# A vision block on one core: the second layer norm's first two groups ahead of the last third of the attention, the queries and keys of the second attention in 222 and 370 columns, unrotated scores first for four images

## The reference, cut to what matters

```python
h = tok(x)                                    # ternary weights, 8-bit activations
y = layernorm(h); q, k, v = split(y @ Wqkv)   # 16 heads of 16
num = exp(rotate(q) @ rotate(k).T / 4)        # rotated queries and keys
den = sum(exp(q @ k.T / 4))                   # unrotated ones, over all keys
h = h + where(causal, num / den, 0) @ v @ Wout + bout
x2 = layernorm(h)
q, k, g = x2 @ w_q, x2 @ w_k, sigmoid(x2 @ w_gate)   # 8 heads of 64, 8 experts
gm = one_hot(argmax(g)) * g
values = sum over e of gm[e] * (x2 @ value_experts[e])
o = softmax(causal(q @ k.T / 8)) @ values
h = h + sum over e, heads of (gm[e] * o) @ output_experts[e]
```

## Time and profile before

| | |
|---|---|
| runs | 240.1, 241.33, 242.55 us |
| profiled execution | 240.91 us, its span 238.4 us |
| PE busy | 207.9 us (87%) |
| DVE busy | 178.7 us (75%) |
| ACT, POOL busy | 93.7 and 79.5 us |
| mean granted clock of TensorE | 0.979 of full speed |

### The profile page before, as it was taken

The page is one execution under the profiler, slowest core; times in us unless marked ns, Lnnn a source line. Parts: engine busy times, 40 slices in busy tenths (PEclk is TensorE's granted clock), DMA queues, the critical chain, the costliest instruction groups (busy, mean ns, idle before and its releaser), DMA issues.

```text
span 238.4 us, 5151 instructions
## 1 busy us (share of the span) xinstructions
PE 207.9 (87%) x2079; PEld 179.6 (75%) x2079; DVE 178.7 (75%) x324; ACT 93.7 (39%) x184; POOL 79.5 (33%) x82
## 2 busy tenths in 40 slices
PE   0153969689979799999999999999999999999994
PEld 0033849688865689987677777778989999999993
DVE  1679895998977767933558666775799979979972
ACT  3578739958741335445332155156202022110000
POOL 8562677000443424002253564955661000000000
PEclk9999999979999679999999999999999999999999
DMA  6998000000000010001602006067005435532102
GB/s 177 265 302 322 2 0 4 0 3 3 3 3 3 18 71 3 0 0 29 252 3 88 3 12 254 0 181 201 3 7 185 120 123 172 165 95 61 44 0 103
DMA packets 7181, 19.56 MB, mean 82 GB/s; under 512 B 1043, under 2 KB 1878, under 8 KB 7030
## 3 DMA queue, kind: packets, MB, share of 16 engines
q1 hardware_dynamic: 7158, 19.24, 26.3%
HBM read 18.55 MB, written 0.68 MB: 81 GB/s over the span
## 4 chain that ended last, share of the span: by engine, by line
PE 49%; DVE 28%; issue 9%; ACT 4%; POOL 4%; DMA 4%; SPq 1%; DVEq 0%; ACTq 0%; POOLq 0%
PE ps L265 13%; PE ps L266 11%; PE ps L267 11%; DVE gx L1101 7%; DMA tw<-tok_weight 4%; PE ps L1233 3%; PE ps L1274 2%; PE ps L1434 2%; DVE oelo L1075 2%; DVE rden L930 2%; DVE amax L774 1%; PE ps L1404 1%; ACT ptb L720 1%; DVE stat L803 1%; POOL velo L485 1%
## 5 line engine op out<-in xcount | busy, mean ns | idle before, releaser
L1101 DVE TENSOR_TENSOR gx<-maskb,oT 128x1184 fp32r<-128x1184 bf16 x31 | 42.3, 1414 | 0.6 <-PE ps L267 0.6
L1038 DVE COPY_PREDICATED v<-onehot,ps 128x512 f32<-128x512 uint8 (+3 forms) x40 | 25.7, 661 | 17.6 <-PE ps L267 17.3
L265 PE MATMUL ps<-gx,oelo 128*128 128x296 f32 x124 | 37.8, 305 | 0.6 <-DVE gx L1101 0.6
L267 PE MATMUL ps<-gx,oehi 128*128 128x296 f32 x124 | 37.2, 300 | 0.0
L266 PE MATMUL ps<-gx,oehi 128*128 128x296 f32 x124 | 37.0, 298 | 0.0
L265 PE MATMUL ps<-vehi,x2lo 128*128 128x512 f32 (+3 forms) x90 | 35.2, 392 | 0.0
L266 PE MATMUL ps<-velo,x2hi 128*128 128x512 f32 (+3 forms) x90 | 33.3, 370 | 0.0
L267 PE MATMUL ps<-vehi,x2hi 128*128 128x512 f32 (+3 forms) x90 | 33.2, 369 | 0.0
L485 POOL TENSOR_TENSOR velo<-veraw,vehi 128x1024 fp32r<-128x1024 f32 x8 | 19.1, 2390 | 23.8 <-ACT vehi L657 17.3
L265 PEld LDWEIGHTS ps<-gx,oelo 128*128 128x128 f32 x124 | 23.3, 188 | 1.8 <-issue 1.3
L266 PEld LDWEIGHTS ps<-gx,oehi 128*128 128x128 f32 x124 | 23.4, 189 | 0.0
(11 more groups left out here) (165 smaller groups left out, 479.8 us busy)
## 6 DMA issues: line engine op xcount, KB each, us to landing
maskb<-mask_rows SPq DMA_DIRECT2D x32, 148.0 KB, 3.9
veraw<-value_w SPq DMA_DIRECT2D x8, 512.0 KB, 3.7
oeraw<-output_w SPq DMA_DIRECT2D x8, 512.0 KB, 4.0
xp<-x_rows SPq DMA_DIRECT2D x6, 336.0 KB, 9.9
w2raw<-w_qkgate SPq DMA_DIRECT2D x1, 1088.0 KB, 14.1
tw<-tok_weight SPq DMA_DIRECT2D x1, 768.0 KB, 8.4
wqraw<-w_qkv SPq DMA_DIRECT2D x1, 768.0 KB, 12.0
out<-yo SPq DMA_DIRECT2D x4, 148.0 KB, 1.9
```

Source lines behind the costliest of these rows:

```text
L265: pe.matmul(o, llo, rhi, start=start, stop=False)
L267: return pe.matmul(o, lhi, rhi, start=False, stop=stop)
L1038: dve.copy_predicated(v2[0:m, t, h0:h1], bcast(onehot[0:m, t, h0:h1, e], 2, DH2), ps[0:m, JBANK[n], 0:(h1 - h0) * DH2].rearrange("p (a b) ...
L1101: dve.tensor_tensor(gx[:, k % NGR].rearrange("p a b t -> p a (b t)"), bcast(maskb[:, w % NMR, k % MEU], 1, 2), oT[:, c % 2].bitcast(F32), ...
```

## The change

The diff, cut to its core; the line numbers in it are not those of the profile.

```diff
+        def unit(b, kind):
+            return 2 * b + (kind if b else 1 - kind)
...
-        NOP = (NB - 1) * BI * S // R
-        OPB = [(4 + g // 2, g % 2 * D) if g < NOP else (1, (g - NOP) * D) for g in range(G)]
-        D_ORDER = [("turn", 0), ("turn", 1), ("turn", 2), ("gate", 0), ("qk", 0), ("out", 4), ("out", 5),
-                   ("qk", 1), ("turn", 3), ("qk", 2), ("qk", 3), ("turn", 4), ("qk", 4), ("turn", 5),
-                   ("gate", 1), ("qk", 5), ("qk", 6), ("gate", 2), ("qk", 7), ("gate", 3), ("qk", 8),
-                   ("gate", 4)]
-        D_ORDER += [("qk", n) for n in range(9, 4 * C2)]
+        EARLY = 2
+        FRONT = EARLY * R
+        QKT = [slice(0, FRONT), slice(FRONT, T)]
+        NQ2 = 2 * C2
+        QKB = [(7, 0, 1)[n % 3] for n in range(NQ2)] + [4 + n % 4 for n in range(NQ2)]
+        OPB = [(7, 0), (7, D), (4, 0), (4, D), (6, 0), (6, D)]
+        OP_AFTER = [2, 2, 3, 3, NB, NB]
+        DENB = [5, 7, 5, 5]
+        D_ORDER = [("pv", NB - 1), ("turn", 0), ("turn", 1), ("qk", 0), ("qk", 1), ("den", NB - 1), ("out", 2), ("out", 3),
+                   ("qk", 2), ("qk", 3), ("out", 4), ("out", 5), ("qk", 4), ("turn", 2), ("qk", 5), ("qk", 6),
+                   ("turn", 3), ("qk", 7), ("gate", 0), ("gate", 1), ("turn", 4), ("gate", 2), ("turn", 5),
+                   ("qk", 8), ("gate", 3), ("qk", 9), ("gate", 4)]
+        D_ORDER += [("qk", n) for n in range(10, 2 * NQ2)]
...
+            for n in range(2):
+                pool.wait_ge(sm["rope_t"], RSTEPS * (n + 1))
+                w2_lo(n)
+            pool.wait_ge(sm["en_ready"], 2)
+            w2_lo(2)
             pool.wait_ge(sm["en_ready"], 2 * 2)
-            w2_lo(0)
-            pool.wait_ge(sm["en_ready"], 2 * 3)
-            w2_lo(1)
-            pool.wait_ge(sm["yT_ready"], 2)
-            w2_lo(2)
             w2_lo(3)
...
-            for n in range(NPJ - 2):
+            for n in range(NPJ - 3):
                 proj_read(n)
+            exps(0, 1)
+            proj_read(NPJ - 3)
+            exps(0, 0)
+            proj_read(NPJ - 2)
+            proj_read(NPJ - 1)
             def ve_hi(e):
                 act.wait_ge(ve_in[e % NVR], 16 * (e // NVR + 1))
@@ -657,13 +674,11 @@
                 act.activation(vehi[:, e % NVR], veraw[:, e % NVR], ACT.Copy).then_inc(sm["vehi_ready"], 1)
             for b in range(NB):
-                exps(b, 0)
-                if b == 0:
-                    proj_read(NPJ - 2)
-                    proj_read(NPJ - 1)
-                exps(b, 1)
-                if b < NVR:
-                    ve_hi(b)
...
+                if b:
+                    exps(b, 0)
+                    exps(b, 1)
+                if 1 <= b <= NVR:
+                    ve_hi(b - 1)
...
-            for b in range(1, NB - 1):
-                causal(b)
-                denominators(b - 1)
-                normalise(b - 1)
-            denominators(NB - 2)
-            normalise(NB - 2)
-            causal(NB - 1)
+            causal(1)
+            denominators(0)
+            normalise(0)
+            causal(2)
+            denominators(1)
+            normalise(1)
+            causal(3)
...
             ln_apply(1, 1)
             x2_lo(0)
+            x2_lo(1)
+            denominators(2)
+            normalise(2)
+            denominators(3)
+            normalise(3)
+            residual(2)
             ln_apply(1, 2)
-            x2_lo(1)
+            residual(3)
             x2_lo(2)
-            denominators(NB - 1)
-            normalise(NB - 1)
-            residual(3)
             ln_apply(1, 3)
             residual(4)
+            x2_lo(3)
             residual(5)
             ln_apply(1, 4)
-            x2_lo(3)
             ln_apply(1, 5)
             x2_lo(4)
             x2_lo(5)
...
+                u = unit(b, kind)
+                if kind:
+                    pe.wait_ge(sm["keys_zero"], 1)
+                    pe.wait_ge(sm["act_read"], act_reads(PJ.index(("qk", late - 1, KC - 1, 1))))
+                else:
+                    pe.wait_ge(sm["keys_zero"], 2)
+                    pe.wait_ge(sm["rope_t"], RSTEPS * KC * late)
+                if u == 0:
                     bank_free(NEARLY - 1)
                 for t in range(2):
-                    if b + kind:
-                        pe.wait_ge(sm["exp_ready"], 4 * b + 2 * kind + t - 1)
+                    if u:
+                        pe.wait_ge(sm["exp_ready"], 2 * u + t - 1)
...
+                if b == NB - 1:
+                    pe.wait_ge(sm["rden_ready"], NB - 1)
+                pe.wait_ge(sm["exp_ready"], 2 * unit(b, 1) + 2)
...
                 if b == 0:
+                    scores(0, 1)
+                    scores(0, 0)
                     proj_job(NPJ - 2)
                     proj_job(NPJ - 1)
+                    denominators(0)
+                    continue
+                scores(b, 0)
+                if b == 1:
+                    attend(0)
                 else:
                     denominators(b - 1)
+                if b == NB - 1:
+                    for g in range(EARLY):
+                        out_proj(g)
                 scores(b, 1)
-                if b == NB - 1:
-                    out_proj(0)
-                    out_proj(1)
-                    denominators(b)
-                    for g in range(2, NOP):
-                        out_proj(g)
-                attend(b)
+                if b < NB - 1:
+                    attend(b)
...
+                before = [m for m in range(n) if QKB[m] == QKB[n]]
+                if before:
+                    pe.wait_ge(sm["qk2_ready"], before[-1] + 1)
+                elif QKB[n] == 7:
+                    pe.wait_ge(sm["h1_ready"], EARLY)
+                elif QKB[n] < 2:
+                    pe.wait_ge(sm["exp_ready"], 4 * NB)
+                elif QKB[n] == 4:
+                    pe.wait_ge(sm["h1_ready"], 2 * EARLY)
+                elif QKB[n] == 5:
                     pe.wait_ge(sm["yT_ready"], NB)
                 else:
-                    pe.wait_ge(sm["qk2_ready"], n - 3)
+                    pe.wait_ge(sm["h1_ready"], G)
                 base = (NQ if kind == "k" else 0) + c * P
-                tc = slice(hf * HALF, (hf + 1) * HALF)
-                pe.wait_ge(sm["x2lo_ready"], 3 if hf == 0 else G)
+                tc = QKT[hf]
+                pe.wait_ge(sm["x2lo_ready"], G if hf else EARLY)
```

More of the change, by code:

```diff
@@ L183, in vit_block @@
         yT = sbuf(proj, "yT", [P, KC, TP], F32, "right")
+        ed = sbuf(proj, "ed", [QR, RT, KC, BI, JS, S], F32, "right")
         en = sbuf(proj, "en", [QR, 2, 2, RT, KC, 2, JS, S], F32, "right")
-        ed = sbuf(proj, "ed", [QR, RT, KC, BI, JS, S], F32, "right")
         proj.close()
@@ L212, in vit_block @@
         ptb = sbuf(last, "ptb", [P, NT, NH2, TI_MAX, S])
-        yo = sbuf(last, "yo", [P, KC, 2, HALF])
         qk = ExitStack()
@@ L217, in vit_block @@
         qk.close()
+        yo = sbuf(last, "yo", [P, KC, 2, HALF])
         NOR, NOE = 4, 2
@@ L486, in ve_lo @@
                                    ALU.subtract).then_inc(sm["velo_ready"], 1)
-            for g in range(GI):
+            for g in range(EARLY):
                 rstd_of(1, g)
-            pool.wait_ge(sm["x2lo_ready"], GI)
+            pool.wait_ge(sm["x2lo_ready"], EARLY)
             ve_lo(0)
-            for g in range(GI, G):
+            for g in range(EARLY, G):
                 rstd_of(1, g)
@@ L681, in qk2_evac @@
                 act.wait_ge(sm["qk2_ps"], n + 1)
-                src, col = ps[:, 4 + n % 4, 0:HALF], slice(hf * HALF, (hf + 1) * HALF)
+                col = QKT[hf]
+                src = ps[:, QKB[n], 0:col.stop - col.start]
                 if kind == "k":
@@ L929, in denominators @@
                 dve.wait_ge(sm["den_ps"], b + 1)
-                dve.reciprocal(rden[:], ps[:, 5 + 2 * (b % 2), 0:UN * S]).then_inc(sm["rden_ready"], 1)
+                dve.reciprocal(rden[:], ps[:, DENB[b], 0:UN * S]).then_inc(sm["rden_ready"], 1)
             def normalise(b):
@@ L1243, in attend @@
                         pe.wait_ge(sm["en_ready"], 2 * b + ii // 2 + 1)
-                    if b == NB - 1 and ii == 2:
-                        turn_x2(0)
                     for c in range(KC):
@@ L1260, in denominators @@
                 for j in range(JP):
-                    ins = pe.matmul(ps[32 * j:32 * j + 32, 5 + 2 * (b % 2), 0:UN * S], cols("blk2", QR),
+                    ins = pe.matmul(ps[32 * j:32 * j + 32, DENB[b], 0:UN * S], cols("blk2", QR),
                                     ed[:, j // JS, :, :, j % JS], start=True, stop=True)
@@ L1265, in out_proj @@
             def out_proj(g):
-                if g < NOP:
+                if g == 0:
                     pe.wait_ge(wout_in, 16)
-                    pe.wait_ge(sm["yT_ready"], NB - 1)
-                else:
+                elif g == G - 1:
                     pe.wait_ge(sm["yT_pad"], 1)
-                    pe.wait_ge(sm["yT_ready"], NB)
```

(41 more changed lines are left out.)

10 lines of the change are left out of this document (2 added, 8 removed).

## The result

The changed kernel takes 250.28 us (median of 4 runs, 249.92 to 252.57) against 240.72 us (median of 4, 238.61 to 242.55): **4.35% slower**, ratio 1.0435 with an interval of 1.0358 to 1.0511. The ratio leaves out executions more than 1.5% above the fastest of their kernel; by the medians it is 4.0%. The forecast was 241.4 us, no change.

A forecast was written before the change was run, and what follows sets the result against it. No engine was taken to bound the whole; DVE bounds the first attention, PE the stretch from 59.15 us. From 240.91, minus 1.2 for earlier value jobs, plus 0.6, 0.7 and 0.4 for clock falls: 241.4 us, no change; range 239.1 to 243.6.

The forecast's parts named there:

- two signs of being wrong: Forecast is wrong if DVE isn't full in the first attention, or if `x2_lo(5)` comes 2 us from 91.4.
- Front: Start of the attention: unrotated scores first let the fourth rotation start at 53.87 instead of 54.41, gaining 0.54 us on DVE.
- First residual at 69.15: Behind the two-group output projection: first residual starts at 69.15 instead of 72.43, 3.3 us earlier.
- clock term (a): PE lull from 56.5 to 59.1 us: a clock fall costs 0 to 1.7 us, taken as 0.6.
- clock term (b): PE lull from 71.6 to 76.6 us, short transposes and two jobs: costs 0 to 1.7 us, taken as 0.7.
- Four groups behind it: Groups 2 to 5 behind the last normalisation: `x2_lo(5)` ends at 91.4 instead of 91.83, 0.4 us of gain left.
- Tail: Behind `x2_lo(5)`, 8 jobs of 370 columns and 2 gate jobs: 9.5 us, value jobs at 100.9 instead of 102.14.
- clock term (c): PE lull from 86.6 to 91.5 us, gate jobs and transposes: costs 0 to 1.7 us, taken as 0.4.
- Rival 4: First attention: `w2_lo` steps collide with the rotations, 3 x 0.42 us on a full DVE; 242.7 us, chance 0.08.
- Rival 3: Every PE lull costs the clock in full, 1.1 to 1.7, 0.9 and 1.7 us; 244.0 us, chance 0.12.
- Rival 1: The clock holds in all three PE lulls; 239.7 us, chance 0.25.
- The sum of 1.2 us: Whole stretch ahead of the value jobs: they start at 100.9 instead of 102.14, 1.2 us earlier, before clock costs.

The follow-up runs named there:

- experiment 8: Kernel before with unused 512-column matmuls in its own lulls, ten ahead of the first scores, eight among transposes, gate and query jobs: 238.28 us, ratio 0.9925.
- experiment 9: Changed kernel with the old attention front and unused matmuls in all its lulls: 238.78 us, ratio 0.994.
- experiment 10: Changed kernel with all three PE lulls filled by unused matmuls, run once more: 238.81 us, ratio 0.9953.
- experiment 4: Kernel before with the new front of the attention alone: 246.95 us, ratio 1.0231.
- experiment 5: Changed kernel with fourteen unused 512-column matmuls right behind `attend(1)`, inside the low stretch: 248.24 us, ratio 1.0325.
- experiment 1: Changed kernel with ten unused 512-column matmuls in PE's wait ahead of `attend(1)`: 241.81 us, ratio 1.004.
- experiment 7: Changed kernel with 22 unused 64-column matmuls ahead of `attend(1)` instead of ten of 512: 246.54 us, ratio 1.0213.
- experiment 3: Changed kernel with the old front of the attention, rest of the change kept: 243.55 us, ratio 1.0123.
- experiment 6: Changed kernel with three unused 512-column matmuls ahead of `attend(1)` instead of ten: 239.69, 245.42 and 249.23 us.
- experiment 2: Changed kernel with all three PE lulls filled by unused matmuls: 239.07 us, ratio 0.9895.

## Why the prediction was wrong, point by point

- **What bounds the stretch**: right up to `causal(1)`, where DVE was full and PE waited. Behind it PE bounded, as forecast, but so much longer that DVE idled 3.66 and 2.46 us. The prediction's own two signs of being wrong both came: DVE wasn't full, and `x2_lo(5)` came 7 us from 91.4.
- **Front, 0.54 us on DVE**: right in the profile. The run is 0.63 us late from its start (the second rotation begins at 44.45 instead of 43.82), and `causal(1)` starts at 58.90, so 0.6 earlier against that. It was no gain of the order: the idle stretch that it removes was itself a loss to the low level, and a filled kernel before has none (experiments 8 to 10).
- **The wait moves to 56.5, 2.6 us**: right, 57.1 with that start, 2.67 us. (From 51.9 the terms given add up to 56.65; the 0.15 changes nothing.)
- **First residual at 69.15**: 75.72, and 68.70 with the wait filled. This is where it failed.
- **The step that failed: the clock term (a), "it costs between 0 and 1.7 us (3.4 at half speed)"**, taken as 0.6. It cost 5.9 us (75.72 less 0.63 less 69.15). I took the length of the low stretch from the row behind the old wait and didn't ask what ended that one: two dense projections. Behind the new wait stand 13 us of scores, products of the exponentials with the values or with the constants (`en`,`vblk` and `ed`,`cst`), and these did not raise the clock (experiments 4 and 5): it stayed low for 13.7 us, until 1.8 us into the output projection, instead of 3.4. So the upper bound of 1.7 us was no bound. That the wait moves and that the clock can fall behind it was right; the size of the term was wrong. The price of the level was off too: the 2.47 us of the earlier trace rows were partly at full clock; wholly at the low level the scores take 3.00.
- **Two groups' norm, 5.4 us from the first residual to `x2_lo(1)`**: right, 75.72 to 81.1.
- **Late batches, clock term (b)**: `x2_lo(1)` to the last normalisation was put at 5.25 us and took 6.6, so 1.3 instead of 0.7, inside its bounds.
- **Four groups behind it, 11.5 us**: 10.8 (87.70 to 98.46), where experiment 1 has 11.5. Why it is shorter here is not worked out.
- **Tail, 9.5 us, and clock term (c), 0.4 us with a bound of 1.7**: 12.6 us (98.46 to 111.08), so 3.1 for the clock, a stretch of 6.8 us where I had allowed one of 3.4. In experiments 1, 7 and 10, with the full clock there, the tail is the 9.5 us of the sum. This bound failed too, and not by the attention's matmuls: jobs of 370 columns ran in it. Whether this lull is followed by a fall also differs between executions: it is in the changed kernel and in experiments 3 and 5, and it is not in experiments 1, 6 and 7.
- **`w2_lo`**: nothing, as put; its four steps lie where forecast (44.61, 48.92, 54.59, 60.37), and no rotation row beside them is longer than 0.78 (the one of 1.20, at 42.07, lies ahead of them, as before). Rival 4 is out.
- **Rival 3** named the mechanism and the lulls, but stopped at 244.0 us, because it had the same bound in it. **Rival 1** is what a filled kernel does: 239.1 and 238.8 against 239.7 forecast.
- **The sum of 1.2 us** was made against a profile with 10.2 us of low clock in it. A kernel before without those takes 238.28 us (experiment 8), so at equal clock there was no gain to be had. The late batches and four groups behind them, put at 0.4 us of gain to `x2_lo(5)`, cost 2.1 us there.

The Trainium skill (TensorE: Matmul & The Clock Gate, "What's actually happening") says that the default state is the throttled one and activity releases it. The runs agree for the fourteen dense matmuls (experiment 5) and not for the attention's: PE was busy for all of the 18.00 us of experiment 4, and the level came back only after 17.1.

## What to carry to other kernels

A wait on TensorE is priced by what stands behind it: ahead of the projections a wait of 2.5 us cost a low stretch of 3.4 us, ahead of the attention's small matmuls one of 2.7 us cost 13.7 and 17.1 us, until an output projection ran. The length that a profile shows for one place is not a bound for another, not even ahead of wide matmuls (6.8 and 13.6 us in the third lull). Before an order is judged by a hand schedule, take the low stretches out of the profile it is compared with, or fill them in both kernels. And where a wait cannot be removed, unused dense matmuls in it are a cheap test of the clock and can be the cure.

## What the runs showed of the hardware that was not expected

- The low level lasted 13.7 and 17.1 us with PE busy throughout (the changed kernel, experiment 4), and 3.4 us where 512-column or 304-column matmuls ran in it (experiments 3 and 5). With 370-column jobs and 64-column gate jobs in turn it lasted 6.8 us (the changed kernel, experiment 3) and 13.6 us (experiment 5).
- The attention's matmuls kept the full level for 17 us (the kernel before, 53.35 to 70.44) and did not restore it in 11.8 (the changed kernel, 61.0 to 72.8) or in 15 (experiment 4).
- A wait filled with 64-column matmuls, busy 2.64 us, did not hold the clock (experiment 7, one profile); with 512-column ones, 2.56 us, it did (experiments 1, 2 and 10).
- The spread of the kernel before goes with its mean clock: over 23 runs 0.993 at 238.07 us and 0.967 at 242.94. On the chip of experiment 8 its 29 runs spread from 238.25 to 242.96, with its lulls filled 237.36 to 239.6.
